# Attention kernel: value steps copied out of PSUM on ScalarE instead of VectorE, with separate counters for key and value steps

## What is computed

```python
q = split_heads(layernorm(x) @ Wq.T + bq)      # 16 heads of 16
k = split_heads(ctx @ Wk.T + bk)
v = split_heads(ctx @ Wv.T + bv)
attn = softmax(q @ k.T * 4.0)
x = x + (attn @ v).reshape(...) @ Wp.T + bp
```

## Time and profile before

| What | Value |
|---|---|
| Median of 3 runs | 2158.23 us (2157.47 to 2158.29) |
| The profiled execution's own time | 2156.64 us |
| Its span, first to last instruction | 2154.8 us |
| PE matmuls, share of the span | 90% |
| PE weight loads | 83% |
| DVE | 73% |
| ACT | 52% |
| POOL | 27% |
| Mean granted TensorE clock | 0.96 of full |

### The profile page before, as it was taken

How to read it: one execution, slowest core, us unless ns; L and a number is a source line. 1 busy time by engine, 2 the same in 40 slices (tenths; PEclk the granted TensorE clock), 3 DMA queues, 4 the chain that set the end, 5 groups by cost and what they waited for, 6 DMA issues and landing times. The chain is left out here.

```text
span 2154.8 us, 47599 instructions
## 1 busy us (share of the span) xinstructions
PE 1947.6 (90%) x18848; PEld 1795.3 (83%) x18848; DVE 1573.1 (73%) x2965; ACT 1127.9 (52%) x1832; POOL 584.3 (27%) x542
## 2 busy tenths in 40 slices
PE   4599999999999999999999999997088399999998
PEld 2599999999999999999999999996055399999998
DVE  3477777777777777777777777775885657777766
ACT  3165656566565655565655655665132135555552
POOL 1223222332223222332232222310211173333335
PEclk8799999999999999999999999999589599999999
DMA  3666566666566566666666566652501455555523
GB/s 135 163 168 166 147 158 165 156 159 157 151 168 167 146 158 155 169 154 160 148 170 167 150 156 163 155 131 52 192 10 40 144 215 196 198 200 204 196 92 116
DMA packets 165266, 328.36 MB, mean 152 GB/s; under 512 B 58448, under 2 KB 96848, under 8 KB 161616
## 3 DMA queue, kind: packets, MB, share of 16 engines
q1 hardware_dynamic: 162000, 317.28, 53.2%
q0 software_dynamic: 3072, 8.39, 1.2%
HBM read 139.03 MB, written 28.44 MB: 78 GB/s over the span
## 5 line engine op out<-in xcount | busy, mean ns | idle before, releaser
L379 ACT COPY a_pT<-a_pst 128x512 f32<-128x512 f32 x768 | 421.6, 583 | 446.5 <-PE a_pst L594 446.5
L385 ACT ACTIVATE a_probs<-a_probs,a_nmax 128x1601 f32<-128x1601 f32 x256 | 418.7, 1635 | 144.2 <-DVE a_probs L423 144.2
L423 DVE TENSOR_SCALAR_CACHE_REDUCE a_probs<-a_pss 128x1608 f32<-128x1608 f32 x256 | 468.2, 1829 | 20.6 <-PE a_pss L583 15.9
L594 PE MATMUL a_pst<-a_id,a_probs 128*128 128x128 f32 (+1 forms) x3328 | 456.3, 275 | 26.1 <-ACT a_pT L379 24.6
L594 PEld LDWEIGHTS a_pst<-a_id,a_probs 128*128 128x128 f32 (+1 forms) x3328 | 387.2, 140 | 74.4 <-ACT a_pT L379 33.3
L347 POOL TENSOR_TENSOR a_tick<-a_tick 128x1 f32<-128x1 f32 x62 | 12.1, 195 | 992.6 <-DMA a_raw<-in_ctxT 897.7
L352 POOL TENSOR_TENSOR a_clo<-a_raw,a_chi 128x402 fp32r<-128x402 f32 x240 | 247.4, 1062 | 4.8
L583 PE MATMUL a_pss<-a_kst,a_bd 96*128 96x402 f32 x1024 | 240.1, 356 | 8.9 <-DVE a_klo L443 6.8
L543 PE MATMUL a_pso<-a_whi,a_chi 128*128 128x256 f32 x806 | 241.2, 299 | 0.0
L441 DVE TENSOR_SCALAR a_khi<-a_psk,a_bk 128x402 fp32r<-128x402 f32 x250 | 158.9, 636 | 110.6 <-PE a_psk L545 94.3
L545 PE MATMUL a_pso<-a_whi,a_clo 128*128 128x256 f32 x806 | 227.1, 282 | 0.0
(11 more groups left out here) (209 smaller groups left out, 3599.0 us busy)
## 6 DMA issues: line engine op xcount, KB each, us to landing
a_kst<-a_khi SPq DMA_DIRECT2D x1024, 100.5 KB, 2.4
a_kst<-a_klo SPq DMA_DIRECT2D x512, 100.5 KB, 2.3
a_raw<-in_ctxT SPq DMA_DIRECT2D x60, 804.0 KB, 5.6
e_gur<-in_wgu SPq DMA_DIRECT2D x24, 1408.0 KB, 6.1
e_dr<-in_wd SPq DMA_DIRECT2D x24, 768.0 KB, 4.8
e_xb<-rows_scr SPq DMA_DIRECT2D x30, 256.0 KB, 4.8
a_bd<-q_scr SPq DMA_DIRECT2D x192, 32.0 KB, 2.1
rows_scr<-f_zero SPq DMA_DIRECT2D x4, 1408.0 KB, 13.7
```

The costliest lines, as they stand in the source:

```text
L379: nc.scalar.copy(pT[:, p % HALF, 4 * i:4 * i + 4, :], ps_t[:, i % 2, :].rearrange("p (t q) -> p t q", q=P)).then_inc(t_copied_act, 1)
L385: nc.scalar.activation(pr, pr, ACT.Exp, bias=nmax[:, b, p:p + 1], scale=-1.0, accum_out=esum[:, b, p:p + 1]).then_inc(probs_ready, 1)
L423: nc.vector.tensor_scalar(probs[:, p % 2, :].rearrange("p (b k) -> p b k", b=QK), ps_s[:, :, 0:KQ], -1.0, None, ALU.mult, ALU.min, accum_o ...
L594: mm = nc.tensor.transpose(ps_t[0:r, i % 2, (t % 4) * P:(t % 4 + 1) * P], probs[:, p % 2, t * P:t * P + r], id_sb[:])
```

## The change

The value steps' copies move from DVE to ACT (`copy_values`), with the same source, destination and shape. On ACT they stand at the end of a slot, behind the exponentials and the copy of group 2. DVE keeps the key steps (`copy_keys`). The counter `kv_copied` becomes `k_copied` and `v_copied`, and each wait names the one that it needs: before step s of batch n + 1 PE waits for the s // 2 steps of the same kind ahead of it. In the first batch the 7 value copies run on ACT as well.

```diff
--- before.py
+++ after.py
@@ -248,7 +248,7 @@
         const_loaded, first_loaded, ctx_loaded, q_loaded, x_loaded = sem("a_cl"), sem("a_fl"), sem("a_ctxl"), sem("a_ql"), sem("a_xl")
         stacked = [[sem(f"a_st{m}{z}") for z in range(PIECES)] for m in range(NC)]
         w_split, ctx_hi_done, ctx_split, bd_zeroed, ticked = sem("a_ws"), sem("a_ch"), sem("a_cs"), sem("a_bz"), sem("a_tk")
-        kv_filled, k_hi_done, kv_copied = sem("a_kvf"), sem("a_khd"), sem("a_kvc")
+        kv_filled, k_hi_done, k_copied, v_copied = sem("a_kvf"), sem("a_khd"), sem("a_kc"), sem("a_vc")
         s_filled, max_ready, probs_ready = sem("a_sf"), sem("a_mr"), sem("a_pr")
         t_filled, t_copied_act, t_copied_dve = sem("a_tf"), sem("a_tca"), sem("a_tcd")
         own_set, sum_inverse, scale_ready, scale_turned, scale_copied = sem("a_ow"), sem("a_sui"), sem("a_sr"), sem("a_stu"), sem("a_sco")
@@ -272,7 +272,7 @@
 
             def stack_keys(n, m, z):
 
-                sp.wait_ge(kv_copied, STEPS * n + STEP_ORDER.index(("k", m, QK // PIECES * (z + 1) - 1)) + 1)
+                sp.wait_ge(k_copied, KSTEPS * n + QK * m + QK // PIECES * (z + 1))
                 cols = slice(z * SKP // PIECES, (z + 1) * SKP // PIECES)
                 for j in range(HALF):
                     if z == 0 and j > 1 and not (isinstance(n, int) and n == 0):
@@ -378,6 +378,15 @@
                 act.wait_ge(t_filled, TG * g + i + 1)
                 nc.scalar.copy(pT[:, p % HALF, 4 * i:4 * i + 4, :], ps_t[:, i % 2, :].rearrange("p (t q) -> p t q", q=P)).then_inc(t_copied_act, 1)
 
+            def copy_values(n, slot, s, bank):
+
+                act.wait_ge(kv_filled, STEPS * n + s + 1)
+                t = STEP_ORDER[s][1]
+                if t < KT - 1:
+                    nc.scalar.copy(v_sb[:, slot, t:t + 2, :], bank[:, :].rearrange("p (t d) -> p t d", t=2)).then_inc(v_copied, 1)
+                else:
+                    nc.scalar.copy(v_sb[0:KTL, slot, t, :], bank[0:KTL, 0:D]).then_inc(v_copied, 1)
+
             def exponentials(g, b, p):
 
                 act.wait_ge(max_ready, g + 1)
@@ -390,6 +399,8 @@
             act.wait_ge(first_loaded, 16)
             for k in range(NC):
                 nc.scalar.copy(c_hi[:, 0, k, :], first_ctx[:, 0, k, :]).then_inc(ctx0_hi_done, 1)
+            for s in range(1, STEPS, 2):
+                copy_values(0, 0, s, first_banks[s % (QK + 1)])
 
             def body(it, first):
                 for b in range(2):
@@ -405,6 +416,10 @@
                         exponentials(g, b, p)
                         if prev and p % HALF > 0:
                             copy_tiles(g - 1, (p - 1) % PAIRS, 2)
+                        if n < B - 1:
+                            for s in SLOT_STEPS[p]:
+                                if s % 2:
+                                    copy_values(n + 1, 1 - b, s, ps_o)
 
             for it in range(NT):
                 body(it, it == 0)
@@ -423,31 +438,23 @@
                 nc.vector.tensor_scalar(probs[:, p % 2, :].rearrange("p (b k) -> p b k", b=QK), ps_s[:, :, 0:KQ], -1.0, None,
                                         ALU.mult, ALU.min, accum_out=nmax[:, b, p:p + 1]).then_inc(max_ready, 1)
 
-            def copy_step(n, slot, s, bank):
+            def copy_keys(n, s, bank):
 
                 dve.wait_ge(kv_filled, STEPS * n + s + 1)
-                kind, *at = STEP_ORDER[s]
-                if kind == "k":
-                    m, q = at
-                    if q % (QK // PIECES) == 0:
-                        z = q // (QK // PIECES)
-                        if m == 1:
-
-                            dve.wait_ge(stacked[0][z], COPIES * (n + 1))
-                        elif not (isinstance(n, int) and n == 0):
-
-                            dve.wait_ge(stacked[1][z], COPIES * n)
-                    hi, lo = (t[:, q * KQ:(q + 1) * KQ] for t in (k_hi, k_lo))
-                    nc.vector.tensor_scalar(hi, bank[:, 0:KQ], bk_sb[:, m:m + 1], None, ALU.add).then_inc(k_hi_done, 1)
-                    dve.wait_ge(k_hi_done, KSTEPS * n + QK * m + q + 1)
-                    nc.vector.scalar_tensor_tensor(out=lo, in0=bank[:, 0:KQ], scalar=bk_sb[:, m:m + 1], in1=hi.bitcast(F32),
-                                                   op0=ALU.add, op1=ALU.subtract).then_inc(kv_copied, 1)
-                else:
-                    t = at[0]
-                    if t < KT - 1:
-                        nc.vector.tensor_copy(v_sb[:, slot, t:t + 2, :], bank[:, :].rearrange("p (t d) -> p t d", t=2)).then_inc(kv_copied, 1)
-                    else:
-                        nc.vector.tensor_copy(v_sb[0:KTL, slot, t, :], bank[0:KTL, 0:D]).then_inc(kv_copied, 1)
+                _, m, q = STEP_ORDER[s]
+                if q % (QK // PIECES) == 0:
+                    z = q // (QK // PIECES)
+                    if m == 1:
+
+                        dve.wait_ge(stacked[0][z], COPIES * (n + 1))
+                    elif n > 0:
+
+                        dve.wait_ge(stacked[1][z], COPIES * n)
+                hi, lo = (t[:, q * KQ:(q + 1) * KQ] for t in (k_hi, k_lo))
+                nc.vector.tensor_scalar(hi, bank[:, 0:KQ], bk_sb[:, m:m + 1], None, ALU.add).then_inc(k_hi_done, 1)
+                dve.wait_ge(k_hi_done, KSTEPS * n + QK * m + q + 1)
+                nc.vector.scalar_tensor_tensor(out=lo, in0=bank[:, 0:KQ], scalar=bk_sb[:, m:m + 1], in1=hi.bitcast(F32),
+                                               op0=ALU.add, op1=ALU.subtract).then_inc(k_copied, 1)
 
             def copy_tail(g, p):
 
@@ -498,8 +505,8 @@
                 dve.wait_ge(ctx0_hi_done, k + 1)
                 nc.vector.tensor_tensor(c_lo[:, 0, k, :], first_ctx[:, 0, k, :], c_hi[:, 0, k, :].bitcast(F32), ALU.subtract).then_inc(ctx0_split, 1)
             dve.wait_ge(const_loaded, 16 * CONSTS)
-            for s in range(STEPS):
-                copy_step(0, 0, s, first_banks[s % (QK + 1)])
+            for s in range(0, STEPS, 2):
+                copy_keys(0, s, first_banks[s % (QK + 1)])
 
             def body(it, first, last):
                 for b in range(2):
@@ -523,10 +530,12 @@
                         else:
                             steps = SLOT_STEPS[p] if ahead else ()
                             for s in steps[0:1]:
-                                copy_step(n + 1, 1 - b, s, bank_of(s))
+                                if s % 2 == 0:
+                                    copy_keys(n + 1, s, ps_k)
                             copy_tail(g - 1, (p - 1) % PAIRS)
                             for s in steps[1:]:
-                                copy_step(n + 1, 1 - b, s, bank_of(s))
+                                if s % 2 == 0:
+                                    copy_keys(n + 1, s, ps_k)
 
             for it in range(NT):
                 body(it, it == 0, it == NT - 1)
@@ -574,7 +583,10 @@
 
                     pe.wait_ge(x1_ready, it)
 
-                pe.wait_ge(kv_copied, STEPS * n + max(s - 1, 0))
+                if s % 2:
+                    pe.wait_ge(v_copied, VSTEPS * n + s // 2)
+                else:
+                    pe.wait_ge(k_copied, KSTEPS * n + s // 2)
                 step(n, slot, s, bank_of(s))
 
             def scores(b, p):
@@ -626,10 +638,12 @@
             pe.wait_ge(ctx0_split, NC)
             for s in range(STEPS):
                 if s > QK:
-                    pe.wait_ge(kv_copied, s - QK)
+                    freed = s - QK - 1
+                    pe.wait_ge(v_copied if freed % 2 else k_copied, freed // 2 + 1)
                 step(0, 0, s, first_banks[s % (QK + 1)])
 
-            pe.wait_ge(kv_copied, STEPS)
+            pe.wait_ge(k_copied, KSTEPS)
+            pe.wait_ge(v_copied, VSTEPS)
 
             def body(it, first, last):
                 for b in range(2):
@@ -659,9 +673,9 @@
                                     project_out(it - 1)
                                 if ahead and p == HALF:
 
-                                    pe.wait_ge(kv_copied, STEPS * (n + 1) + 6)
+                                    pe.wait_ge(v_copied, VSTEPS * (n + 1) + 3)
                                 elif p == 0:
-                                    pe.wait_ge(kv_copied, STEPS * (n + 1) - 1)
+                                    pe.wait_ge(v_copied, VSTEPS * (n + 1))
                                 else:
                                     pe.wait_ge(o_normed, w)
                                 weigh(g, of, h)
```

## The result

The changed kernel takes 2190.72 us in the median of 4 runs (2188.84 to 2193.22), the kernel before, run beside it, 2158.26 us (2157.47 to 2158.43). The ratio is 1.0152 with a 95% interval of 1.0134 to 1.0169: slower by 32.5 us. The forecast was 2188.9 us.

What follows compares the result with a forecast made beforehand. The prediction took PE's instruction order to bound the kernel. A new wait of 31.0 us less 0.3 us in the first batch gave +30.7 us on 2158.2, so 2188.9 us, 1.4% slower, range 2182 to 2197.

Steps and rivals of the forecast that it cites:

- What bounds the kernel: Attention loop: PE, 98% busy, sets the time by its instruction order; cutting DVE's load by 128.6 us gains nothing by itself.
- Step 9 in slot 5: PE waits 1.07 us for step 7's copy, queued on ACT; 1.00 us stays in each of 31 batches, 31.0 us.
- The other figure for ACT's copy: Step 7's copy on ACT at the skill's 612 ns: an estimated 1.06 us a slot, 32.9 us in sum.
- The cover of the other value steps: Value copies other than step 7's cost nothing; the tightest, step 5's at slot 3's end, has 0.30 us left.
- The first batch: Before the loop: DVE's last key copy no longer stands behind step 13's value copy, first scores 0.34 us earlier, -0.3 us.
- Rival A: Attention loop: DVE holds PE, its relief ends every wait on it; not slower, 2145.6 us; chance 0.03.
- Rival C: Step 9 in the loop: the new idle microsecond also halves PE's clock, 46 us more, 2235 us; chance 0.04.
- The sum: Whole kernel: 31.0 us for step 9's waits less 0.3 us in the first batch, +30.7 us.

Runs made afterwards that it cites:

- run 34: A count, not a label: the kernel before, unchanged, run 34 times beside the experiments; 2158.2 us beside the first four, 2158.3 us beside the others.

## Why the prediction was right, point by point

- **What bounds the kernel.** Right. PE's order sets the time, and DVE's load does not: with all seven value copies off DVE and the new wait avoided, the time is 2160.4 us, with six of them off 2158.6, and neither is under the 2158.2 of the kernel before.
- **Step 9 in slot 5.** The wait was forecast as 1.07 us, 33 us in all, and its net cost as 1.00 us; measured were 1.04 us, 32.1 us in all, and 0.97 us from the slots' lengths. The difference is in two small terms: ACT's second copy starts 0.47 us after the first (530.85, 531.32), not 0.50, and PE resumes 0.05 us after its end, not 0.07. The copy's own 0.57 us was 0.585. The 0.11 us to the load after next was as forecast (531.96, 532.07). 31 x 1.00 = 31.0 was 30.0.
- **The other figure for ACT's copy.** The estimate of 612 ns by the figures of the Trainium skill (ScalarE: Activation LUTs, What ACT_TABLE_LOAD costs) is 5% over the 585 ns measured; the 32.9 us worked out from it is further from the 30.0 of the slots than the sum by rows.
- **The cover of the other value steps.** Right: no wait on `a_v` outside slot 5. The 0.30 us left at the end of slot 3 show in the timeline of the changed kernel:

```profile
520.46 0.56 ACT L379 COPY a_pT<-a_pst 128x512 f32<-128x512 f32 x1
520.93 0.58 ACT L386 COPY a_v<-a_pso 128x512 f32<-128x512 f32 x1
521.84 1.07 ACT L379 COPY a_pT<-a_pst 128x512 f32<-128x512 f32 x2 [0.32 <-PE a_pst L606]
```

ACT is done at 521.51 and idles for 0.32 us before the next turned group is ready.

- **The first batch.** Forecast 0.3 us. The first scores start 0.39 us earlier in the profile (93.92 against 94.31), but that start moves by more between profiles. DVE's last key copy closes up to the one before:

```profile
92.02 0.64 DVE L456 SCALAR_TENSOR_TENSOR a_klo<-a_pss,a_bk,a_khi 128x402 fp32r<-128x402 f32 x1
92.57 0.63 DVE L454 TENSOR_SCALAR a_khi<-a_pss,a_bk 128x402 fp32r<-128x402 f32 x1
```

The clean measure is PE's wait for this copy, just ahead of the first scores. It was 7.12 us before and 7.12 with the two counters alone, and is 6.79 to 6.81 us in the changed kernel and in the four runs with value copies on ACT and the old order of steps: 0.3 us, as forecast.

- **Rival A** (DVE holds PE): its sign for it was the 8% of the loop in which no weights load. Those gaps are still there, 1418 - 1279.3 = 139 us, and a lighter DVE closed none of them: the key wait stayed at 12.6 us. The Trainium skill's advice to judge TensorE's headroom by LDWEIGHTS time (Perfetto Trace Analysis, Identifying the Most-Contended Engine) finds the room; the list of waits says who holds it.
- **Rival C** (clock): the loop's granted clock stayed at 1.00 with a microsecond's wait in each batch. The one fall between first and last scores that its profile has and the one before has not is in the last batch, where no such wait is.
- **The sum** was +30.7 us; the last scores come 30.9 us later. That this is so close is in part luck: slot 5 gave 30.0 us and the start -0.4, and the 1.3 us to 30.9 are the slot of the last batch at the lower clock (0.8 us) and small shifts in the other slots, for which the sum had no term.
- **What lies behind the loop** had no term either. The profiles' spans differ by 33.8 us, 3 us more than the last scores. Of these, 2.4 us are in the stretch from the first load of the circuit block to the first of the experts, 151.6 us before and 154.0 after, though its code is the same. The granted clock tells them apart. The same two pieces of this stretch, 64 to 72 and 72 to 110 us behind its first load, before and then after (columns as in the earlier trace rows):

```profile
1621.18:1629.18 8.00, 7.45 (x13) 2.83 (x14) 7.38 (x33) 4.02 (x8) 1.24 (x1) 0.79 0.19 66
1629.18:1667.18 38.00, 35.05 (x150) 25.11 (x149) 17.49 (x51) 9.13 (x14) 3.26 (x3) 1.00 0.13 42
...
1652.65:1660.65 8.00, 7.71 (x11) 3.02 (x12) 7.38 (x33) 3.08 (x6) 1.24 (x1) 0.60 0.19 66
1660.65:1698.65 38.00, 35.05 (x140) 23.82 (x140) 16.53 (x49) 9.80 (x15) 3.26 (x3) 0.96 0.13 42
```

In these 46 us the rows count 152 loads after, where they count 163 before. Over the ten profiles of this study the stretch took 151.1 to 151.6 us at a mean granted clock of 0.83 or 0.84 (three of them, the kernel before among these), and 153.4 to 154.8 us at 0.81 or 0.82 (the other seven, the run with the two counters alone among them). None was profiled twice, but the kernel before, run 34 times beside the experiments, shows that one kernel varies like this: its 12 runs with a granted clock of 0.961 or more took 2156.9 us in the mean, its 13 with 0.959 or less 2159.3. What decides it in a given run stays open. It has the size of the differences of 1 to 4 us between expected and measured times above.

## What to carry to other kernels

Before a copy is moved to a less busy engine, look at what stands ahead of it there, and at who waits for its bank: a copy of 0.58 us behind 2.1 us of other work cost a full microsecond, and the same copy ahead of that work, still on the less busy engine, cost at most 0.2%. Where one bank is used twice within a slot, the first use has to have left it before PE is back for the second. On a bound engine, read the list of its waits by releaser: it gave a reordering of one line worth 0.5%, which no share of busy time points to.

## What the runs showed that was not expected

The time follows PE's wait almost one to one over a range of 40 us, with ACT idle 44% of the time and DVE a third: the loop's other engines have a great deal of slack, but none of it made up for a wait in PE's order. And a value copy on ACT is shorter than on DVE, 585 against 692 ns for 128x512 elements from PSUM, and 364 against 410 ns for 65x256.
